# Turning the exponentials of a global attention by VectorE blocks and a trip through DRAM, with a second score place and new call orders

## The reference

```python
perceived = conv_general_dilated(x, w_perc, (1, 1), 'SAME', feature_group_count=Cc) + b_perc   # 3x3, depthwise, 3 per channel
hid = gelu(einsum('bphw,dp->bdhw', perceived, w_up1) + b_up1)
x_new = x + einsum('bdhw,cd->bchw', hid, w_up2) + b_up2
x = x_new + local_attn(x_new)                  # 3x3 window, softmax over 9 scores
...
xn = group_norm(x, gamma, beta)                # 8 groups
q, k, v = xf @ Wq + bq, xf @ Wk + bk, xf @ Wv + bv     # xf: 1024 pixels x 128
attn = softmax(einsum('bnc,bmc->bnm', q, k) * scale)   # 1024 x 1024 per image
out = einsum('bnm,bmc->bnc', attn, v) @ Wp + bp
return xn + out
```

## Time and profile before

| | us |
|---|---|
| median of 3 runs (1060.2 to 1060.88) | 1060.43 |
| the profiled execution | 1062.82 |
| its span in the trace | 1060.8 |
| PE busy | 1021.0 (96%) |
| DVE busy | 791.3 (75%) |
| ACT busy | 723.6 (68%) |
| POOL busy | 394.7 (37%) |

### The profile page before, as it was taken

How to read it: one execution, slowest core, us unless ns; L and a number is a source line. 1 busy time by engine, 2 the same in 40 slices (tenths; PEclk the granted TensorE clock), 3 DMA queues, 4 the chain that set the end, 5 groups by cost and what they waited for, 6 DMA issues and landing times.

```text
span 1060.8 us, 21242 instructions
## 1 busy us (share of the span) xinstructions
PE 1021.0 (96%) x7060; PEld 939.6 (89%) x7060; DVE 791.3 (75%) x1628; ACT 723.6 (68%) x1377; POOL 394.7 (37%) x365
## 2 busy tenths in 40 slices
PE   5978999999999999999999999999999999999897
PEld 5857989999998999999899999989999898998776
DVE  6957779777877877788687777868777786777674
ACT  2566767767677776767767776776767677677463
POOL 4635252352515235251523525153351515232031
PEclk9989999999999999999999999999999999999999
DMA  5101010010201001010100101010020100000000
GB/s 91 22 1 21 1 31 11 11 32 1 40 0 30 10 10 30 0 36 4 30 10 0 40 0 30 10 30 10 0 40 0 30 10 10 11 2 11 11 21 21
DMA packets 85493, 18.64 MB, mean 18 GB/s; under 512 B 67536, under 2 KB 85328, under 8 KB 85456
## 3 DMA queue, kind: packets, MB, share of 16 engines
q1 hardware_dynamic: 84608, 17.77, 8.6%
q10 hardware_dynamic: 848, 0.39, 0.2%
HBM read 9.76 MB, written 8.39 MB: 17 GB/s over the span
## 4 chain that ended last, share of the span: by engine, by line
PE 89%; DVE 4%; issue 3%; ACT 2%; POOL 2%; DMA 0%; ACTq 0%; DVEq 0%; POOLq 0%
PE work L468 16%; PE work L470 15%; PE work L469 15%; PE ps_t L622 10%; PE ps_s L468 5%; PE ps_s L470 5%; PE ps_s L469 5%; PE work L540 4%; PE work L561 4%; PE work L596 2%; PE work L527 2%; PE work L549 1%; PE work L586 1%; POOL g_lo L1439 1%; DVE et_lo L1875 1%
## 5 line engine op out<-in xcount | busy, mean ns | idle before, releaser
L1869 DVE TENSOR_REDUCE nm<-ps_s 128x1 f32<-128x1024 f32 x124 | 151.5, 1222 | 78.8 <-PE ps_s L470 75.9
L1439 POOL TENSOR_TENSOR g_lo<-u,g_hi 128x512 fp32r<-128x512 f32 x60 | 78.3, 1306 | 351.0 <-ACT g_hi L969 351.0
L1058 ACT ACTIVATE et_hi<-ps_t 128x1024 fp32r<-128x1024 f32 x128 | 131.2, 1025 | 99.1 <-PE ps_t L622 99.0
L468 PE MATMUL work<-t_lo,wc_hi 128*128 128x256 f32 x576 | 170.3, 296 | 5.9 <-DVE wc_lo L1688 4.4
L1875 DVE TENSOR_TENSOR et_lo<-ps_t,et_hi 128x1024 fp32r<-128x1024 f32 x128 | 156.1, 1219 | 22.6 <-ACT et_hi L1058 21.0
L470 PE MATMUL work<-t_hi,wc_hi 128*128 128x256 f32 x576 | 162.7, 283 | 0.0
L469 PE MATMUL work<-t_hi,wc_lo 128*128 128x256 f32 x576 | 162.1, 281 | 0.0
L1048 ACT ACTIVATE e<-ps_s,nm 128x1024 f32<-128x1024 f32 x124 | 138.2, 1114 | 25.2 <-DVE nm L1869 23.4
L468 PE MATMUL work<-et_lo,vv_hi 128*128 128x256 f32 x512 | 148.6, 290 | 4.6 <-DVE r_tok L1887 3.8
L470 PE MATMUL work<-et_hi,vv_hi 128*128 128x256 f32 x512 | 145.0, 283 | 0.0
L469 PE MATMUL work<-et_hi,vv_lo 128*128 128x256 f32 x512 | 144.7, 283 | 0.0
(11 more groups left out here) (182 smaller groups left out, 2352.1 us busy)
## 6 DMA issues: line engine op xcount, KB each, us to landing
x_in<-in_x SPq DMA_DIRECT2D x64, 128.0 KB, 3.4
out<-r_tok SPq DMA_DIRECT2D x32, 256.0 KB, 2.3
w_up_t<-in_L_conv_w_up SPq DMA_DIRECT2D x1, 384.0 KB, 4.2
y<-in_L_conv_w_qkv SPq DMA_DIRECT2D x1, 192.0 KB, 4.9
const<-in_const ACTq DMA_DIRECT2D x1, 166.0 KB, 5.8
y<-in_L_conv_w_up ACTq DMA_DIRECT2D x1, 128.0 KB, 5.3
const<-in_const ACTq DMA_DIRECT2D x1, 64.0 KB, 3.6
bv_row<-in_L_conv_b_qkv SPq DMA_DIRECT2D x1, 64.0 KB, 2.9
```

Of the source, the lines that this page charges most:

```text
L468: te.matmul(dst, wh, xl, start=first, stop=False)
L1058: act.activation(et_hi[:, :, (t % 4) * 128:(t % 4 + 1) * 128], ps_t[:, :].rearrange("p (k c) -> p k c", k=TILES), ACT.Copy) \
L1439: return pool.tensor_tensor(dst, full, hi, ALU.subtract)
L1869: dve.tensor_reduce(nm1[:, t:t + 1], score_tile(n, t)[:, :], AX.X, ALU.max, negate=True) \
```

## The change

The transposition leaves PE. ACT's `exp` writes to one of two `e`; DVE's new `turn_e` transposes each 32x32 block of it into one of two places `turned`; SP's new `send` writes that to one of four places in DRAM (`spread`, 512 KB a tile), and SP's new `fetch` reads it back in four transfers of 32 partitions, so that the blocks land on the partitions of their keys, into `et_f`. `et_hi_tile` (ACT) now reads `et_f`, and `et_lo_tile` moves from DVE to POOL and writes its result over `et_f`. `probs_t` goes, so `ps_t` becomes a second place for scores. In the diff, cut to its core, `et_lo_tile` is POOL's and `turn_e` DVE's.

```diff
 def score_tile(n, t):
-    return work_all[:, 0:PIX] if is_last(n) and t % 2 else ps_s
+    return ps_t if t % 2 else ps_s
...
+def send(n, t):
+    sp.wait_ge(*e_turned.after(n, t))
+    sp.dma_start(spread[t % 4].rearrange("p i c -> p (i c)"),
+                 turned_both[:, t % 2].rearrange("p i k q -> p (i k q)")).then_inc(e_sent[t % 2].handle, 16)
+
+def fetch(n, t):
+    landed, read = e_sent[t % 2].after(n, t // 2), pe["pv"].after(n, t // 2 - 2)
...
+    sp.wait_ge(*landed)
+    if t % 2 == 0:
+        sp.wait_ge(*read)
...
+    for i in range(4):
+        sp.dma_start(et_f[32 * i:32 * (i + 1), t % 4].rearrange("r s k q -> r s (k q)"),
+                     spread[t % 4, :, i].rearrange("(s r) c -> r s c", s=4)) \
+          .then_inc(e_fetched[t % 4].handle, 16)
...
 def scores(n, t):
...
-    te.wait_ge(*e_ready.after(n, t - 1))
+    te.wait_ge(*e_ready.after(n, t - 2))
...
-def probs_t(n, t):
-    te.wait_ge(*e_ready.after(n, t))
-    te.wait_ge(*et_lo_ready.after(n, t - 1))
-    for kt in range(TILES):
-        mm = te.transpose(ps_t[:, kt * 128:(kt + 1) * 128], e[:, kt * 128:(kt + 1) * 128], ident)
-    mm.then_inc(pe["t"].handle, 1)
...
 def k_half(n, k):
+    act.wait_ge(*pe["as"].after(n - 1, 3))
 def xn_hi_half(n, k):
-    act.wait_ge(*pe["vv"].after(n - 1, 1))
+    act.wait_ge(*pe["qq"].after(n - 1, 1))
+    act.wait_ge(*pe["kk"].after(n - 1, 1))
 def kk_hi_half(n, k):
+    act.wait_ge(*pe["s"].after(n - 1, 7))
 def exp(n, t):
-    act.wait_ge(*pe["t"].after(n, t - 1))
+    act.wait_ge(*e_turned.after(n, t - 2))
 def et_hi_tile(n, t):
-    act.wait_ge(*pe["t"].after(n, t))
...
+    act.wait_ge(*e_fetched[t % 4].after(n, t // 4))
+    act.activation(et_hi[:, t % 4].rearrange("p s k q -> p (s k q)"),
+                   et_f[:, t % 4].rearrange("p s k q -> p (s k q)"), ACT.Copy).then_inc(et_hi_ready.handle, 1)
...
+def et_lo_tile(n, t):
+    pool.wait_ge(*et_hi_ready.after(n, t))
+    minus(et_lo[:, t % 4].rearrange("p s k q -> p (s k q)"), et_f[:, t % 4].rearrange("p s k q -> p (s k q)"),
+          et_hi[:, t % 4].rearrange("p s k q -> p (s k q)").bitcast(F32)).then_inc(et_lo_ready.handle, 1)
...
+def turn_e(n, t):
+    dve.wait_ge(*e_ready.after(n, t))
+    dve.wait_ge(*e_sent[t % 2].after(n, t // 2 - 1))
+    dve.wait_ge(*e_fetched[t % 4].after(n, t // 4 - 1))
+    dve.transpose(turned_both[:, t % 2].rearrange("p i k q -> p k i q"),
+                  e_both[:, t % 2].rearrange("p (k i q) -> p k i q", k=TILES, i=4)).then_inc(e_turned.handle, 1)
```

## The result

The changed kernel takes 1091.1 us (median of 4 runs, 1089.6 to 1094.5), the kernel before beside it 1060.7. The ratio is 1.0287 (95% interval 1.0257 to 1.0316): slower, by 30 us.

A forecast was written before the change was run, and what follows sets the result against it. PE sets the pace; 55.4 plus waits of 4.65, 0.2, 2.1, 0.35 and 2.3 gives 65.0 per turn against 62.3, +32 for twelve. 1060.4 + 32 - 6 = 1087 us, range 1012 to 1118, its own 1065 to 1118.

The forecast's parts named there:

- PE: PE's stream: transposes leaving take 7.0 us off each turn, from 62.3 to 55.4 if nothing waits.
- The collision: POOL's subtractions and DVE's two-SBUF-input instructions never run together; a held DVE instruction waits up to 2.45 us.
- Step (1): From `attended(z,1)`, ending at 6.0, through DVE and ACT: 6.6 us in a row, `et_hi(a,0)` done at 12.65.
- Step (2): POOL's `et_lo` tiles hold the first two of DVE's four combines; `u` is final at 26.0, not 22.4.
- Step (3): From `u` through table load, gelus, `g_hi` and `g_lo`, 5.85 us: `up2(c,0)` starts at 31.85, +4.65 per turn.
- Step (4): POOL's list running on to 43.9: `values(a,2)` +0.2, `v(c,1)` +2.1, `k(c,1)` +0.35 us per turn.
- Step (5): End of turn, `row_max(b,0)` behind alternating POOL and DVE calls: `scores(b,2)` waits 1.0 to 3.8, taken as 2.3 us.
- Fill and drain: The run's two ends: 28 us of PE work go but trips lie bare; taken as -6 us, bounds -20 and +5.
- the trip through DRAM: A tile's send and fetch: 7 to 8 us, counted as covered by two to three tiles between.
- rival (C): A tile's trip takes 15 us as transfers queue, `et_hi(a,0)` at about 20: 1165 us; chance 0.02.
- Rival (A): Collisions hold only the combines, later steps have room: turn 60.2, 1029 us (1005 to 1055); chance 0.29.
- rival (E): The forecast plus PE's clock falling each turn at the wait before `up2`, +20 us: 1107 us; chance 0.17.

The follow-up runs named there:

- e6: The changed kernel with zeros written for most of POOL's `et_lo` and `gelu` put ahead of `et_hi(a,3)` on ACT: 1001.0 us, ratio 0.9430.
- e1: The changed kernel with POOL writing zeros to 1016 of 1024 columns of `et_lo` instead of subtracting: 1060.0 us, ratio 0.9986.
- e5: The kernel before, without seven of the eight transposes of each tile from the second image on: 1006.5 us, ratio 0.9483.
- e11: The lists of e8 with ACT's `exp(b,0)` ahead of `et_hi(a,7)` and DVE's `row_max(b,1)` right behind `row_max(b,0)`: 1037.8 us, ratio 0.9779.
- e8: The lists of e7 with three more calls moved, ACT's `q_half(c,1)`, PE's `v(c,0)` and DVE's `transform_even(d)`: 1045.5 us, ratio 0.9849.
- e7: The changed kernel, whole computation, lists reordered: `gelu` ahead of `et_hi(a,3)`, `et_lo(a,2)` waiting for the combines, other calls moved: 1045.7 us, ratio 0.9841.

## Why the prediction was right

The time was forecast at 1087 and measured at 1091; the turn at 65.0 and measured at 65.1. By its steps:

- **PE**: the transposes left, but they were worth less than 7.0. In e6, with a clock of 1.00 and 1.6 of waits, PE is busy 56.3 per turn (619.77 us in eleven turns): 5.9 less than before. So the 55.4 was too low by 0.9.
- **DVE, ACT, POOL**: `turn_e` 1.23 (1.30 was taken), `et_hi` 1.06 (1.03), `et_lo` 2.40 in the median and 2.50 in the mean (2.45). All within their bounds.
- **The collision**: right in mechanism and size. In e1, with the reads gone, `combine` is back at 690 ns; with them it has a mean of 1921. Two of the four combines are held, as forecast, though the second and third and not the first two.
- **Step (1)**: `et_hi(a,0)` done at 12.65; measured 13.1 (760.36 less 747.22). But what it waited for last was its fetch (0.63), which the step has not in it.
- **Step (2)**: `u` final at 26.0; measured 26.2.
- **Step (3)**: `up2` at 31.85; measured 31.5, from other parts. The table load, 1.28 in the sum, was done before `u` was final and cost nothing, so the second `g_lo` ends at 30.7; the last 0.8 is PE's, late with `values` and `local_values` at the lower clock. The place of the wait was wrong: it stands before `values(a,0)`, because the bank of `conv(c,4)` passes to it, which I had overlooked. Had `values` not waited, `up2` would have.
- **Step (4)**: 0.2 before `values(a,2)` came out as nothing, 2.1 before `v(c,1)` as 1.05, 0.35 before `k(c,1)` as nothing, and 0.75 before `group_moments` was not foreseen: the 128x1 instruction that makes `moments` has two SBUF inputs and waits for POOL too (1.14 at 781.34, beside `g_lo`).
- **Step (5)**: 2.3 before `scores(b,2)`, taken as near the middle of 1.0 to 3.8 with no reason for the place, so this closeness is luck; measured 2.1, by `transform_ends` in front of `row_max(b,0)`.
- **Fill and drain**: -6 was taken; 1092.7 - 12 x 65.12 = 311.3 against 313.2 is -2.

**The sum** came out to 0.1 per turn by luck. The forecast's waits, 4.65, 0.2, 2.1, 0.35 and 2.3, are 9.6; measured are 6.9. PE's busy time was taken as 55.4; measured is 58.3, of which 1.6 is the clock's (below). Two misses, of 2.7 and 2.9, cancel.

**The term that was mis-sized** is the trip through DRAM. It was costed at 7 to 8 us and at nothing on the path. Page part 6 has the landings near the estimate,

```profile
spread<-turned SPq DMA_DIRECT2D x128, 512.0 KB, 3.0
et_f<-spread SPq DMA_DIRECT2D x512, 128.0 KB, 3.5
```

but tile 3 took 9.34 from its send's issue to `et_hi`, and SP sent it 1.84 after `turn_e` was done (758.7), as it was still issuing a fetch: 11.2 in all. "The lists put two to three tiles between" was then no cover, for `gelu` and `exp` stand behind `et_hi` on ACT. Since this ended at the same time as the collision, the collision's part of the sum came out right with one of its two causes missing. The sign named for rival (C), `et_hi` idle behind a DMA, is in the trace as well as those of the forecast (130.5 us). Rival (C) had put the point from which the trip decides at about 10 us; with 11.2 it does hold `gelu`, but at the same place of the turn as the collision and not on top of it. Rival (A), 1029, took it that the later steps had room: they had not.

**The clock**, rival (E): it was right that it falls in each turn. In the 5 us at this place of the turn it is 0.66 in eleven of twelve turns and 0.71 in one. The window of the change that begins with `values(a,0)`:

```profile
772.89:777.89 5.00, 5.00 (x28) 5.00 (x29) 4.68 (x7) 4.35 (x8) 2.49 (x3) 0.66 0.27 108
```

From 772.89 on `values(a,0)` and `local_values(b,1)` take 4.23 and 1.61, where they took 2.93 and 1.33: 1.6 us. But `up2` could not have begun before the second `g_lo`, which ended at 777.93, and began at 778.73: by these rows only the last 0.8 of it is on the path, some 10 us for twelve turns and not 20. No run held the clock up by itself.
The rule of the Trainium skill that the prediction cited (TensorE: Matmul & The Clock Gate, HAM oscillation — how this bites in real kernels) is borne out in that the fall returns with each turn; the 1107 that it would have given was too much by the part that other waiting hides.

What stays open: why the transposes took only 5.9 of PE's busy time with them (5.0 of 6.1 in e5); and the 0.4 by which 58.3, less the clock's 1.6, is above the 56.3 of e6. The first matmul after each wait is longer in the rows, but I did not measure that by itself. Why e11 gains 8 us in its runs while its profiled turn is as long as that of e8 is open in part: the profile of e11 is of the slowest of its five runs (1042.7), and its span is 4 us shorter than e8's.

## What to carry to other kernels

When work leaves the engine that sets the pace for one that has room, look at what the new place shares with its neighbours and at what stands behind it in each list: here the room of POOL was real in us and useless in place. An edit that brings nothing may be one of two limits that end together; only the pair of edits shows it (31 and 0 us alone, 90 together). In a fixed list, a call that waits for a transfer should stand behind all calls that do not need it.

## What was not expected of the hardware

- An instruction on 128x1 elements on DVE took 2.23 us beside a subtraction of POOL, and both ended at 791.0. Over the whole run it has a mean of 1717 ns; in the kernel before it is (group of DVE)

```profile
L1838 DVE TENSOR_TENSOR gn<-cols,gn 128x1 f32<-128x1 f32 x16 | 2.5, 159 | 0.7 <-POOL gn L1477 0.7
```

So here the wait was for POOL's whole instruction, whatever the size of DVE's own.

- A zero-writing POOL instruction of 1.79 us did not hold DVE's combines (e1, 690 ns).
- The clock fell to 0.66 behind waits of 2.66 in the change and 2.35 in e8, shorter than the 3.5 that the drain of before had shown, and in e7 behind two waits of 0.84 and 0.96 close together, while it stayed at 1.00 behind the 2.10 before `scores(b,2)` in the change (in the 5 us from 808.91 on). PE's timeline and a window of e7:

```profile
643.23 0.93 PE L648 MATMUL work<-kp,q_c 128*128 128x204 f32 x4 [0.84 <-ACT q_c L1048]
645.13 0.68 PE L576 MATMUL ps_s<-kk_lo,qq_hi 128*128 128x512 f32 x1 [0.96 <-ACT e L1116]
```

and the window:

```profile
645.00:650.00 5.00, 4.87 (x16) 3.91 (x17) 4.92 (x17) 2.98 (x9) 1.35 (x1) 0.66 0.26 105
```
